# Spectral filters on TensorE: four far blocks as three products, two filters side by side, taps stacked, loops written out

## The reference, cut to what matters

```python
U_plus  = causal_conv(phi, u)                  # 16 filters k, along time, per channel
U_minus = causal_conv(phi, u * sgn) * sgn      # sgn = +1, -1, +1, ...
out  = einsum('btkd,k,kde->bte', U_plus,  sigma ** 0.25, Mpp)
out += einsum('btkd,k,kde->bte', U_minus, sigma ** 0.25, Mpm)
for i in range(3):                             # three taps
    out += einsum('btd,de->bte', shift(u, i), Mu[i])
```

## Time and profile before

| | us |
|---|---|
| median of 3 runs | 1483.65 |
| lowest, highest | 1482.17, 1483.76 |
| span of the profiled execution, first to last instruction | 1477.3 |
| spectral stage, window in that execution | 584.1 |

### The profile page before, as it was taken

One profiled execution on the slowest core, in us unless ns is written; L12 is line 12 of the kernel. 1 busy time (PEld: TensorE's weight loads), 2 busy tenths in 40 slices (PEclk: granted clock), 3 DMA queues, 4 the chain that ended last, 5 costly groups with the idle time before them and its releaser, 6 DMA issues. The chain is left out here.

```text
span 1477.3 us, 31682 instructions
## 1 busy us (share of the span) xinstructions
PE 1340.9 (91%) x12866; PEld 856.7 (58%) x12866; DVE 606.5 (41%) x942; ACT 589.5 (40%) x1029; POOL 163.2 (11%) x178
## 2 busy tenths in 40 slices
PE   8999978888987999998899999999999999948767
PEld 5323357777776788887555555555555555536544
DVE  4981131111113677775432332333333333335652
ACT  3986742225576455454422222222222222223440
POOL 4000019600002222221000000000000000003000
PEclk9879979999998899999999999999999999979977
DMA  4900000000005000000000000000000000040001
GB/s 108 115 1 1 1 4 0 0 0 0 0 0 198 33 4 4 4 4 3 1 0 0 0 0 0 0 0 0 0 0 0 0 0 0 0 115 1 1 1 58
DMA packets 34319, 24.19 MB, mean 16 GB/s; under 512 B 24653, under 2 KB 28781, under 8 KB 34237
## 3 DMA queue, kind: packets, MB, share of 16 engines
q1 hardware_dynamic: 33853, 21.92, 6.7%
q10 hardware_dynamic: 384, 1.07, 0.3%
HBM read 20.80 MB, written 2.18 MB: 16 GB/s over the span
## 5 line engine op out<-in xcount | busy, mean ns | idle before, releaser
L1130 PE MATMUL sp_f<-hankel,sp_ut 128*128 x2304 | 420.9, 344 | 0.0
L1130 PEld LDWEIGHTS sp_f<-hankel,sp_ut 128*128 128x128 f16 x2304 | 222.8, 98 | 216.7 <-issue 27.5
L1169 ACT COPY sp_sums<-sp_f 64x1023 f32<-64x1023 f32 x128 | 129.0, 1008 | 426.7 <-PE sp_f L1130 426.7
L1192 DVE COPY sp_sums<-sp_f 64x1024 f32<-64x1024 f32 x128 | 155.3, 1213 | 91.8 <-PE sp_f L1130 91.8
L1190 DVE COPY sp_mix<-mix 128x512 f32 x64 | 27.3, 427 | 280.7 <-PE sp_f L1130 280.7
L1141 PE MATMUL sp_o<-sp_sums,sp_mix 128*64 128x128 f32 (+2 forms) x1024 | 123.6, 392 | 0.0
L502 PE MATMUL convv<-runningv,toeplitz 128*128 128x128 f32 x610 | 85.7, 287 | 15.1 <-DVE runningv L519 15.1
L502 PEld LDWEIGHTS convv<-runningv,toeplitz 128*128 128x128 f32 x610 | 74.2, 191 | 26.6 <-DVE runningv L519 26.6
L502 PE MATMUL convh<-runningh,toeplitz 128*128 128x128 f32 x610 | 84.0, 284 | 4.5 <-DVE runningh L519 1.3
L1141 PEld LDWEIGHTS sp_o<-sp_sums,sp_mix 128*64 128x64 f32 x1024 | 63.2, 134 | 37.4 <-issue 15.4
L502 PEld LDWEIGHTS convh<-runningh,toeplitz 128*128 128x128 f32 x610 | 74.0, 191 | 13.3 <-DVE runningh L519 13.3
(11 more groups left out here) (311 smaller groups left out, 1888.3 us busy)
## 6 DMA issues: line engine op xcount, KB each, us to landing
hankel<-phi_rows SPq DMA_DIRECT2D x32, 256.0 KB, 6.5
ex_w<-in_L_ffn_weight SPq DMA_DIRECT2D x1, 2080.0 KB
m_plus<-in_L_ffn_M_phi_plus SPq DMA_DIRECT2D x2, 1024.0 KB, 14.2
m_minus<-in_L_ffn_M_phi_minus SPq DMA_DIRECT2D x2, 1024.0 KB, 16.5
out<-x SPq DMA_DIRECT2D x8, 256.0 KB, 3.4
x<-in_x ACTq DMA_DIRECT2D x2, 512.0 KB, 7.6
x<-in_x SPq DMA_DIRECT2D x2, 512.0 KB, 9.0
ar<-in_L_ffn_M_u SPq DMA_DIRECT2D x2, 192.0 KB, 3.5
```

The costliest lines, as they stand in the source:

```text
L1130: mm = nc.tensor.matmul(f_ps[b][:, lo:(half + 1) * BANK], ut[:, hu, b, i, :, :].rearrange("p a c -> p (a c)"), m.hankel[:, hf, ds(j * 2 + ...
L1169: nc.scalar.copy(sums[n][HALF[1], b, 1:T], f_ps[b][HALF[1], 0:T - 1]).then_inc(f_act, 1)
L1192: nc.vector.tensor_copy(sums[n][HALF[0], b, :], f_ps[b][HALF[0], :]).then_inc(f_dve, 1)
```

## The change

With tokens u0 to u3 and blocks H0 to H3, the far part of ranges 2 and 3 was H2 u0 + H1 u1 and H3 u0 + H2 u1. Now one shared product P = H2 (u0 - u1) serves both: range 2 takes (H1 + H2) u1 + P, range 3 takes (H2 + H3) u0 - P. That needs a fifth token set, u0 - u1 (`du`, made by GpSimd), and a second table of sums, `hankel_sum`, whose rows `weights_stage` makes on GpSimd and which SP loads beside `spectral_norm_stage`; the first table is cut to three spans (`NEAR`). P stays in a PSUM bank of its own, ScalarE copies it to `shared`, and VectorE adds or subtracts it as it evicts ranges 2 and 3; ScalarE evicts ranges 0 and 1.

Two filters go side by side: every product now has 512 columns, 256 of each of two filters, and each of the four ranges a bank of its own with both filters in it, with its own pair of semaphores. `sums` has one buffer for both filters; mixing goes in two parts, first the segments that need ranges 0 and 1, then the long one. The mixing weights are read from `m.mix` where they lie, without the copy to `mixk`.

The taps are stacked: tap 0 on the lower and tap 1 on the upper 64 partitions, then tap 2 alone, in two passes instead of three. `apart` (now filled by GpSimd) holds each image's tokens twice, once a token late. Both loops are written out. The tokens of the next images are transposed within the loop, in three parts at pairs 2, 4 and 6, into a bank of their own (`t_ps`) and two buffers `ut`. The taps come between the products and the mixing of the first pair.

```diff
+NEAR = 3 * SPAN
+PHI_ROW = SPAN + 2 * NEAR
...
+    PARTS = ((0, 1), (2, 3), (4,))
+    TURN_AT = (2, 4, 6)
...
+        ut = [sb(f"sp_ut{k}", [P, PIECES16, 2, SETS, 2, C], F16) for k in range(2)]
+        sums = sb("sp_sums", [P, 2, 2, T])
+        shared = [sb(f"sp_shared{k}", [P, 2, SPAN]) for k in range(2)]
+        y_ps = [pb(f"sp_y{r}", [P, 2, SPAN]) for r in range(SPANS)]
+        p_ps = pb("sp_p", [P, 2, SPAN])
+        t_ps = pb("sp_t", [P, BANK])
...
             @block.gpsimd
...
+                nc.gpsimd.memset(ar[:, :, :, :], 0.0).then_inc(zero, 1)
+                nc.gpsimd.memset(apart[:, :, :], 0.0).then_inc(zero, 1)
+                for g in range(G):
+                    source = m.normed[:, g * TILES:(g + 1) * TILES, :].rearrange("p n t -> p (n t)")
+                    if g:
+                        pool.wait_ge(ut_ok, len(PARTS) * g)
+                    nc.gpsimd.tensor_copy(u[:, ::-1], source).then_inc(u_ok, 1)
+                    nc.gpsimd.tensor_tensor(du[:, ::-1], source[:, 0:SPAN], source[:, SPAN:2 * SPAN], ALU.subtract).then_inc(u_ok, 1)
...
+                    for b in range(2):
+                        for late in range(2):
+                            first = AR - 1 + late
+                            nc.gpsimd.tensor_copy(apart[HALF[late], b, first:], source[HALF[b], 0:T - late]).then_inc(apart_ok, 1)
...
+                def product(out, g, j, b, s, table, lo, first, last):
+                    for n, (hu, hf) in enumerate(PRODUCTS):
+                        mm = nc.tensor.matmul(out[:, :, :], ut[g % 2][:, hu, b, s, :, :].rearrange("p a c -> p (a c)"),
+                                              table[:, hf, 2 * j:2 * j + 2, lo:lo + SPAN],
+                                              start=first and n == 0, stop=last and n == len(PRODUCTS) - 1)
+                    return mm
+                def filtered(g, j, b):
...
+                    taken(y_c[0], 2)
+                    product(y_ps[0], g, j, b, 0, m.hankel, 0, True, True).then_inc(y_ok[0], 1)
+                    taken(y_c[1], 2)
+                    product(y_ps[1], g, j, b, 0, m.hankel, SPAN, True, False)
+                    product(y_ps[1], g, j, b, 1, m.hankel, 0, False, True).then_inc(y_ok[1], 1)
+                    taken(p_c, 1)
+                    product(p_ps, g, j, b, SPANS, m.hankel, 2 * SPAN, True, True).then_inc(p_ok, 1)
+                    if g == 0 and b == 0 and j % 2 == 0:
+                        pe.wait_ge(m.sum_in[j // 2], 16 * PIECES16 * 4)
+                    taken(y_c[2], 2)
+                    product(y_ps[2], g, j, b, 1, m.hankel_sum, 0, True, False)
+                    product(y_ps[2], g, j, b, 2, m.hankel, 0, False, True).then_inc(y_ok[2], 1)
+                    taken(y_c[3], 2)
+                    product(y_ps[3], g, j, b, 0, m.hankel_sum, SPAN, True, False)
+                    product(y_ps[3], g, j, b, 2, m.hankel, SPAN, False, False)
+                    product(y_ps[3], g, j, b, 3, m.hankel, 0, False, True).then_inc(y_ok[3], 1)
...
+                def mixed(g, j):
+                    pairs = g * KP + j + 1
+                    pe.wait_ge(y_c[0], 4 * pairs)
+                    pe.wait_ge(y_c[1], 4 * pairs)
+                    for some in ((2, 1, 0), (3,)):
+                        if some == (3,):
+                            pe.wait_ge(y_c[2], 4 * pairs)
+                            pe.wait_ge(y_c[3], 4 * pairs)
+                        for n in range(2):
...
+                for g in range(G):
+                    for j in range(KP):
+                        for later in parts_at(g, j):
+                            turn(*later)
+                        filtered(g, j, 0)
+                        filtered(g, j, 1)
+                        if j == 0:
+                            autoregressive(g)
+                        mixed(g, j)
             @block.scalar
...
+                        for b in range(2):
+                            done = (g * KP + j) * 2 + b
+                            if b == 0 and done:
+                                act.wait_ge(mix_ok, g * KP + j)
+                            for r in range(2):
+                                act.wait_ge(y_ok[r], done + 1)
+                                for a in range(2):
+                                    to, of = summed(r, a)
+                                    nc.scalar.copy(sums[HALF[a], :, b, to], y_ps[r][HALF[a], :, of]).then_inc(y_c[r], 1)
+                            act.wait_ge(p_ok, done + 1)
...
+                            nc.scalar.copy(shared[done % 2][:, :, :], p_ps[:, :, :]).then_inc(p_c, 1)
             @block.vector
...
+                            dve.wait_ge(p_c, done + 1)
+                            for r, op in ((2, ALU.add), (3, ALU.subtract)):
+                                dve.wait_ge(y_ok[r], done + 1)
+                                for a in range(2):
+                                    to, of = summed(r, a)
+                                    nc.vector.tensor_tensor(sums[HALF[a], :, b, to], y_ps[r][HALF[a], :, of], shared[done % 2][HALF[a], :, of], op).then_inc(y_c[r], 1)
...
+                pool.wait_ge(pstep, 6)
+                nc.gpsimd.tensor_tensor(both[:, :], phi_n[:, 0:NEAR], phi_n[:, SPAN:T], ALU.add).then_inc(both_ok, 1)
+                pool.wait_ge(both_ok, 1)
+                nc.gpsimd.tensor_copy(phi_t[:, 0, far], both[:, :]).then_inc(both_ok, 1)
+                pool.wait_ge(both_ok, 2)
+                nc.gpsimd.tensor_tensor(phi_t[:, 1, far], both[:, :], phi_t[:, 0, far], ALU.subtract).then_inc(both_ok, 1)
...
+def hankel_sum_load(nc, m, phi_rows, sp):
+    for k in range(FILTERS):
+        for piece in range(PIECES16):
+            src = bass.AP(phi_rows.tensor, (k * PIECES16 + piece) * PHI_ROW + SPAN + NEAR + 2, [[2, P], [1, 2 * SPAN]])
+            sp.dma_start(m.hankel_sum[:, piece, k, :], src).then_inc(m.sum_in[k // 4], 16)
```

More of the change, by code:

```diff
@@ L1068, in out_of @@
+        y_ok = [sem(f"st_range{r}") for r in range(SPANS)]
+        y_c = [sem(f"st_range_taken{r}") for r in range(SPANS)]
         def out_of(lo, cnt, par):
@@ L1071, in out_of, with turned, tokens, parts_at @@
             return o_ps[HALF[par], half, :, first:first + cnt // 2]
[L1073 to L1078, removed]
+        def turned(g, part):
+            bank = t_ps[:, :] if g or part == 0 else o_ps[:, part - 1, :, :].rearrange("p b n -> p (b n)")
+            n = len(PARTS[part])
+            return bank[:, 0:n * SPAN].rearrange("p (i a b c) -> p b i a c", i=n, a=2, b=2)
+        def tokens(g, piece, part):
+            some = PARTS[part]
+            return ut[g % 2][:, piece, :, some[0]:some[-1] + 1, :, :]
+        def parts_at(g, j):
+            if g == 0 and j == -1:
+                return [(0, part) for part in range(len(PARTS))]
+            return [(g + 1, TURN_AT.index(j))] if j in TURN_AT and g + 1 < G else []
+        def summed(r, a):
+            lo = r * SPAN + a
+            hi = min(lo + SPAN, T)
+            return slice(lo, hi), slice(0, hi - lo)
         with nc.Block() as block:
@@ L1118, in _ @@
                     mm.then_inc(ar_ok, 1)
[L1120 to L1133, removed]
@@ L1145, in _ @@
[L1145 to L1149, removed]
+                def mixed(g, j):
[7 more added lines that the diff above has]
+                        for n in range(2):
+                            for seg in some:
+                                lo, cnt = SEGMENTS[seg]
+                                for par in range(2):
+                                    mm = nc.tensor.matmul(out_of(lo, cnt, par), m.mix[:, 2 * j + n, SCALES - 1 - seg, par, :], sums[:, n, :, lo + par:lo + cnt:2],
+                                                          start=False, stop=False, skip_group_check=True)
+                    mm.then_inc(mix_ok, 1)
@@ new lines, in _ @@
+                pe.wait_ge(first_ok, 1)
+                for part in range(len(PARTS)):
+                    turn(0, part)
+                pe.wait_ge(m.table_in, 16 * PIECES16 * FILTERS)
+                for g in range(G):
[7 more added lines that the diff above has]
+                        mixed(g, j)
@@ L1202 @@
 HEAD_DIM = C // HEADS
-TILES = T // P
 def norm_stage(nc, m, tag):
@@ L1899, in hybrid_program @@
         m.x_in = [sem(f"x_in{q}") for q in range(2)]
+        m.sum_in = [sem(f"sums_in{q}") for q in range(FILTERS // 4)]
         phi_rows = nc.dram_tensor("phi_rows", (FILTERS, PIECES16, PHI_ROW), F16).ap()
```

179 lines of the change are left out of this document (90 added, 89 removed).

## The result

The change is faster: 1429.22 us median (1427.87 to 1434.73, 4 runs) against 1482.91 of the kernel before (1479.17 to 1483.76, 4 runs, three of them those of the first table), ratio 0.9661 with a 95% interval of [0.9639, 0.9683] (the quotient of the two medians is 0.9638). Predicted were 1432 us in a range of 1422 to 1446. The profiled span went from 1477.3 to 1426.1 us, 51.2 us less; the sum had said 51.3.

The account below looks back on a forecast made before the run. The prediction took TensorE to bound the rewritten stage; 9.45 + 497.3 + 15.0 + 4.8 = 526.6 us against 577.9, 51.3 less, so 1483.65 - 51.3 = 1432 us, range 1422 to 1446.

Parts of the forecast that it names:

- pairs: TensorE's filter products and mixing in the rewritten stage: 15.54 us a pair, 32 of them 497.3 us, 539.2 before.
- taps: TensorE's taps in two stacked passes, 32 records for 48: 3.75 us, four times 15.0, VectorE's additions covered by products.
- transposes: Ten for eight inside the loop: 1.6 us, three times 4.8; cast and subtraction cost nothing, 3 us without cover.
- start: Stage start to first product 7.85 us, plus 1.6 for the low clock: 9.45 in all, bounds 7.9 and 11.
- The sum for the kernel before: Old stage from start to last mixing: 10.70 us, 32 x 16.85, and 10.39 + 2 x 8.81 at loop ends, 577.9.
- the low clock at the start: TensorE's first products: 1.6 us charged, from 0.64 of transposes and 0.92 of taps before.
- if the clock leaves 1.00 inside the stage: A sign in the profile after, on TensorE's granted clock, that would show the prediction wrong.
- Evictions: Second half of mixing waits for VectorE's last two sums: 1.6 us under 1.88 of cover, cost nothing, slack 0.27.
- SP: SP's 32 transfers of 128 KB inside the norm stage: taken as 0, 2.8 us at 0.64 each, far bound 9.
- (b): Rival: SP outlasts the norm stage, 1435 us at 0.64 each, 1441 at the far bound; chance 0.10.
- (c): Rival: writing out the loop gains by itself, 27.5 us of weight-load "issue" returning, 1405 us; chance 0.02.
- (d): Rival: VectorE's last sums late every pair, 1456 us, chance 0.04; with the clock falling too, 1506, chance 0.06.

Follow-up runs that it names:

- The first experiment: Far blocks as four products again, ten block products a unit for nine, no sum table, against the kernel after: 1468.12 us, 0.9908 of the kernel before.
- the fourth: Taps in three passes, 48 records for 32 in each group of images, against the kernel after: 1436.35 us, 0.9690 of the kernel before.
- the third: Each product of 512 columns cut into two of 256, one per filter, against the kernel after: 1430.91 us, 0.9657 of the kernel before.

## Why the prediction was right

**The sum held in all terms but one.** Predicted and measured: pairs 497.3 and 496.8; taps 15.0 and 14.9 (before, 25.0 for all four by spacing); transposes 4.8 and 4.5; start 9.45 and 7.86 + 2.84 = 10.7. That is 526.6 and 526.9. So close a sum is in part luck: the start is 1.25 too short, and the other three terms are together 0.9 too long. The sum for the kernel before, 577.9, is 1.0 short of the 578.9 measured, since it took every mixing at the 3.76 us of the first turn, and by spacing they were 3.76 to 3.91. So the stage fell by 52.0 us and not 51.3; it also starts 0.45 us later, and what follows it took 0.4 longer, which leaves the span's 51.2. The first experiment confirms the price of the block products and the fourth that of the stacking (7.4 us); the third says that of the products' gain only some 4 us come from wider matmuls.

**One term was mis-sized: the low clock at the start**, 1.6 us charged, 14.60 - 11.76 = 2.84 paid. Taken literally, the prediction's sign "if the clock leaves 1.00 inside the stage" came true there, in the first 5.8 us of products and nowhere behind them. The low clock is not a fixed price. Kernels with the very same start had first products of 14.3 to 14.6 us in six profiles and of 13.1 in two, a cost of 1.3 to 2.84 us; 1.6 lies inside that scatter. The Trainium skill (TensorE: Matmul & The Clock Gate, Part 1) says that the slow beginning varies from run to run; these rows agree.

**The covers held, and were worth more than the text said.** Transposes "nothing, 3 us without the cover": right at nothing, but 6.2 us and a lowered clock without it, since the three parts share one bank and queue behind VectorE's additions (waits of 3.03 and 1.49 us at the first change), which the prediction left out. Evictions "slack 0.27 us": 0.25 by the experiments. SP: 1.3 us of margin beside the spectral norm stage, so 0 was right, but not by much: in two of the later kernels that stage took 16.0 us for 17.3, and SP's issues ended 0.1 us before its last copy and 0.06 us after it. The other table was the nearer miss, and the prediction did not look there: its rows went from 2 KB to 1.5, and its 32 issues from 17.23 to 19.29 us. They end at 479.26, GpSimd's last copy in that norm stage at 479.00, so a fraction of a microsecond is all it cost; in the other kernels with this table SP ended at most 0.9 us behind the copy.

**The rivals.** (b) did not come at 32 issues: SP took 15.99 us for rows of 1 KB where rows of 2 KB had taken 17.23, so the overhead that spoke for it does not show in SP's time. It came at 64. (c) is refuted: the loops written out alone gave 1.0001. The rule on taken branches of the Trainium skill (Runtime: NRT & Kernel Launch, Instruction fetch mechanics) brought nothing here: 27.5 us of "issue" with and without loops. (d) had its place and its price right, but its second half is refuted for this wait: 28 waits of 1.6 us did not lower the clock, so 1506 could not have come that way, and even three sums too many only reach level with before. The chance given to it was too high.

**The remaining 2.8 us** between 1432 and 1429.22 have no cause in the stage: the span fell by what was forecast, and the kernel's own runs differ by 6.9 us. The prediction and the text ahead of it took the 6.4 us between the profiled span and the median of before for time outside the span. That is wrong: wherever a run's span is on record, the run is 1.7 to 1.9 us longer (once 2.2), so the profiled execution of before was one of the quicker ones. The forecast needs only the difference of the stages and does not hang on it.

## What to carry to other kernels

Where one engine is fully busy at one clock, count its columns: here the saving was the columns not computed, and neither the loops nor the matmuls' width added much. Before adding work to an engine that is half idle, look for the one moment when the busy engine waits on it; the slack there (0.25 us) counts, not its average load. After such a change look again at the start of the stage: clearing buffers ahead of the first needed copy cost 2.2 us here, and waiting for more than the first products need 2.0.

## What the hardware showed unexpectedly

SP's time for 32 table issues does not fall with the bytes. Rows of 2 KB took 17.23 to 17.81 us (three kernels), rows of 1.5 KB 18.23 to 19.87 (eleven), rows of 1 KB, beside another stage, 15.72 to 16.13 (ten), and 64 issues of 64 rows of 1 KB 41.34. In the traces of before and after, most issues start 0.47 to 0.49 us behind the one before at every one of these sizes; what differs is a few long ones, over 0.6 us three times at 2 KB, seven times at 1.5 KB and once at 1 KB, the longest 1.63. The half issues start 0.64 us apart. What makes an issue long, and one of half the rows dearer than a whole one, was not tried.

Idle time and clock: 28 waits of 1.6 us left the granted clock at 1.00, of three waits of 3.0 us two were followed by the lower level, and so were all three stretches of 7.6 to 8.0 us with 2.1 us of work in them.
